# Two-layer graph attention: the first layer's value products split over two column tiles of 64 queries

## What is computed

```python
kc = k.reshape(B, H, Nc, CHUNK, Dh)          # B 8, H 4, Nc 8, CHUNK 256, Dh 64
vc = v.reshape(B, H, Nc, CHUNK, Dh)
scores = jnp.einsum('bhnd,bhjcd->bhnjc', q, kc) / sqrt(Dh)
scores = jnp.clip(scores, -10.0, 10.0)
scores = jnp.where(mask == 0, -10.0, scores)
attn = jax.nn.softmax(scores, axis=-1)
ctx = jnp.einsum('bhnjc,bhjcd->bhnd', attn, vc)
```

## Time and profile before

| what | value |
|---|---|
| runs of the kernel before | 4877.83 and 4884.79 us, median 4881.31 |
| profiled execution, first to last instruction (span) | 4877.6 us |
| TensorE busy, matmuls / weight loads | 4739.8 us (97%) / 4347.8 us (89%) |
| VectorE / ScalarE / GpSimd busy | 84% / 61% / 15% |
| granted TensorE clock, mean | 0.995 of 2.4 GHz |
| first layer | from the start to about 3390 us |
| second layer | the rest, about 1490 us |

### The profile page before, as it was taken

How to read it: one execution, slowest core, us unless ns; L and a number is a source line. 1 busy time by engine, 2 the same in 40 slices (tenths; PEclk the granted TensorE clock), 3 DMA queues, 4 the chain that set the end, 5 groups by cost and what they waited for, 6 DMA issues and landing times. The chain is left out here.

```text
span 4877.6 us, 136121 instructions
## 1 busy us (share of the span) xinstructions
PE 4739.8 (97%) x56349; PEld 4347.8 (89%) x56349; DVE 4078.2 (84%) x9728; ACT 2977.2 (61%) x3317; POOL 738.5 (15%) x613
## 2 busy tenths in 40 slices
PE   7999999999999999999999999997899999999999
PEld 5998899898899988989888998996899999999998
DVE  5888788787788877878877887787899999999999
ACT  5444444444444444444444444443899999999998
POOL 3121121111121211211211211011000110100100
PEclk9999999999999999999999999999999999999999
DMA  5100100001010001000001000010321221221221
GB/s 113 53 18 18 31 27 19 23 18 27 19 31 18 18 23 27 27 15 27 20 17 32 27 18 18 21 36 22 105 79 31 76 79 31 76 79 31 76 66 38
DMA packets 173916, 186.82 MB, mean 38 GB/s; under 512 B 7520, under 2 KB 157408, under 8 KB 173152
## 3 DMA queue, kind: packets, MB, share of 16 engines
q1 hardware_dynamic: 166192, 159.49, 11.9%
q0 software_dynamic: 7088, 18.36, 1.6%
HBM read 110.43 MB, written 38.03 MB: 30 GB/s over the span
## 5 line engine op out<-in xcount | busy, mean ns | idle before, releaser
L785 ACT ACTIVATE slot<-slot,shift 128x1024 f32<-128x1024 f32 x1024 | 1113.5, 1088 | 1568.7 <-PE slot L638 1568.7
L648 PEld LDWEIGHTS outs<-v_s,probs 128*128 128x128 f32 x16384 | 1974.5, 192 | 106.3 <-issue 29.7
L648 PE MATMUL outs<-v_s,probs 128*128 128x128 f32 x16384 | 1988.3, 275 | 0.0
L921 DVE SCALAR_TENSOR_TENSOR probs<-slot,bound 128x1024 f32<-128x1024 f32 x1024 | 1250.3, 1223 | 368.9 <-ACT slot L785 365.3
L1555 ACT ACTIVATE u<-s_all,d_sign 128x1024 bf16<-128x1024 f32 x1024 | 1117.1, 1138 | 56.9 <-PE sums L1456 39.5
L637 PE MATMUL slot<-q_hl,k_hl 128*128 128x512 f32 x2048 | 895.2, 437 | 18.5 <-DVE probs L921 9.9
L638 PE MATMUL slot<-q_hl,k_hl 128*128 128x512 f32 x2048 | 802.7, 392 | 0.0
L941 DVE SCALAR_TENSOR_TENSOR ctx_sum<-outs,inv,ctx_sum 128x64 f32<-128x64 f32 x3584 | 770.0, 278 | 31.7
L1452 PE MATMUL sums<-x_mixed,u 128*128 128x130 f16 x8192 | 785.5, 219 | 3.7 <-issue 3.5
L1456 PE MATMUL sums<-x_mixed,mask 128*128 128x65 f16 x8192 | 759.4, 193 | 5.5 <-issue 5.5
L1687 DVE TENSOR_TENSOR u<-u,mask 128x1024 f16<-128x1024 bf16 x1024 | 694.3, 689 | 76.6 <-ACT u L1555 67.6
(11 more groups left out here) (156 smaller groups left out, 3678.5 us busy)
## 6 DMA issues: line engine op xcount, KB each, us to landing
q_hl<-q_hl SPq DMA_DIRECT2D x128, 256.0 KB, 3.7
s_all<-s_turned SPq DMA_DIRECT2D x64, 512.0 KB, 5.7
x_q_s<-in_x SPq DMA_DIRECT2D x32, 512.0 KB, 4.6
x<-y SPq DMA_DIRECT2D x32, 512.0 KB, 3.2
t_o_s<-x SPq DMA_DIRECT2D x16, 1024.0 KB, 5.5
out<-t_o_s SPq DMA_DIRECT2D x16, 1024.0 KB, 6.9
x_q_s<-x SPq DMA_DIRECT2D x28, 512.0 KB, 5.8
probs<-in_adj POOLq DMA_DIRECT2D x12, 512.0 KB, 8.4
```

The source lines that it names most:

```text
L648: end = nc.tensor.matmul(outs[i % OUTS][:, q, :], probs[:, i % PROBS, r, q * P:(q + 1) * P], v_s[:, c * JC + r, h * E1:h * E1 + P], start= ...
L785: nc.scalar.activation(slot[:, :, :], slot[:, :, :], ACT.Exp, bias=shift[:, 0:1], scale=SCALE).then_inc(act_done, 1)
L921: nc.vector.scalar_tensor_tensor(probs[:, i % PROBS, :, :], spot(kind, "step", s, i)[:, :, :], P_LOW, bound[:, (i // H) % 2, :, :], ALU.ma ...
```

## The change

Each of the 8 products of `values` becomes two. The stationary operand is now 64 of the 128 queries, and the result goes to partitions 0 to 63 of `outs` for the first half and 64 to 127 for the second, which are two column tiles of TensorE's array. Each of the two streams the same 128 columns of `v_s`, as the one did before (`V_COLS` = `P` = 128). What is computed, where it lands and all waits and signals stay as they were; the signal is still on the last matmul of the step. The number of matmuls of `values` doubles, in the order tile, half of the chunk, half of the queries.

```diff
+V_COLS = P
...
-        v_w = H * E1 + P - E1
+        v_w = H * E1 + V_COLS - E1
...
                     for q in range(IT):
                         for r in range(JC):
-                            end = nc.tensor.matmul(outs[i % OUTS][:, q, :], probs[:, i % PROBS, r, q * P:(q + 1) * P],
-                                                   v_s[:, c * JC + r, h * E1:h * E1 + P],
-                                                   start=(r == 0), stop=(r == JC - 1))
+                            for g in range(2):
+                                rows_of = slice(g * D, (g + 1) * D)
+                                end = nc.tensor.matmul(outs[i % OUTS][rows_of, q, 0:V_COLS],
+                                                       probs[:, i % PROBS, r, q * P + g * D:q * P + (g + 1) * D],
+                                                       v_s[:, c * JC + r, h * E1:h * E1 + V_COLS],
+                                                       start=(r == 0), stop=(r == JC - 1))
                     end.then_inc(probs_used, 1)
```

## The result

The changed kernel takes 5186.51 us (runs of 5185.37 and 5187.66), the kernel before 4881.31: a ratio of 1.0622, 95% interval 1.0602 to 1.0642. That is slower by 305 us. The profiled execution is the one of 5185.37 us; its span is 5183.5.

What follows compares the result with a forecast made beforehand. The prediction took TensorE's matmul stream in the first layer as the bound. 4881 + 68 (an extra slot per step) + 336 (array emptying at grouping changes) = 5285 us, +8.3%; range 4830 to 5830.

Steps and rivals of the forecast that it cites:

- TensorE bounds the first layer, the load sets the pass: First layer: TensorE's stream sets the time; loading 128 fp32 weights decides each value pass, 0.1117 us, by 3 ns over streaming.
- The halves' streams overlap: Value products: both array halves work side by side, so 32 passes need the time of 16 slots of 0.109 us.
- rival C: Value passes: the two halves don't overlap at all, +1.70 us per step, 6623 us; chance 0.12.
- 17 slots per step: Value block: in-order starts and no overlap on one half add a slot; +0.066 us per step, +68 us.
- Loads, at nothing: Value weight loads: 64-column loads hide behind another stream; bounds 0 and 0.15 us per step, taken as 0.
- Rival B: Value loads wait for the matmul before them: +0.90 us per step, 5803 us without emptying; chance 0.11.
- Regrouping, 0.328 us per step: Between scores and values: the array empties at two grouping changes per step, 0.162 + 0.166 us, +336 us in all.
- Rival A, no emptying: Between scores and values: grouping travels with each instruction, costing no drain; 4949 us, or 4837 without a lost slot; chance 0.34.
- The range of the likeliest case: Whole kernel, halves side by side with emptying, chance 0.40: 5090 to 5454 us.
- half of the tails missing: Grouping changes between scores and values: the assumption given for the 5090 us lower end, only part of the emptying paid.

Runs made afterwards that it cites:

- the pairs: Scores of two steps issued, then values of two steps, on the kernel before with nothing split: 4927.73 us, ratio 1.0092.

## Why the prediction was right, and where it was not

The forecast was 5285 us (+8.3%) with a range of 4830 to 5830; measured were 5187 (+6.2%). The sign and the range held, the mechanism (two halves side by side, paid for with two changes of grouping per step) held, and the forecast was 98 us too high. That it came this near is in part luck: inside the largest term two errors cancel.

- *TensorE bounds the first layer, the load sets the pass.* Right: 65 columns in place of 128 change nothing while the load is whole (+0.2%).
- *The halves' streams overlap* (against rival C). Right: 32 passes in 16 slots, and 0.109 us per slot in the run with the block twice.
- *17 slots per step.* Wrong, and this is the failed step: "Matmuls start in order here" does not hold between the halves. The block has 16 slots, as the timeline shows. The term was +0.066 us per step; measured, it is 16 x (0.109 - 0.1117) = -0.04, or -0.048 with the 0.1087 us used in the expectations. The difference, 0.11 us x 1024 = some 115 us, is the whole error and a little more.
- *Loads, at nothing.* Right: pairs start 0.109 us apart, as if no load were there, except for the 0.05 us of each block's first pair, and with 65 columns the interval falls to 0.058 us, which loads one behind the other would not allow (0.118 by the prediction's 59 ns each). Rival B, loads waiting for the matmul before them in program order, is out.
- *Regrouping, 0.328 us per step.* The size came out well, 0.346, which is 354 us in place of 336. The makeup was off. I had priced the whole time until the last results land (0.162 us from scores to values, 0.166 back, beyond the usual next start) and let the load stand ready. The rows show a shorter emptying, 0.09 us in either direction (0.32 - 0.23 and 0.20 - 0.11), and a load that is not ready: it starts only afterwards, 0.05 us for 64 columns and 0.1 for 128. Two errors of opposite sign, and the near hit of the term is luck.
- *Rival A, no emptying*, on which I had put 0.34, rested on L719, a 64-column operand right behind whole value passes without a gap. The profile after shows what that row is:

```profile
3686.97 0.11 PEld L723 LDWEIGHTS slot<-ident,sd 128*64 128x64 f32 x1 [0.17 <-issue]
3686.97 0.30 PE L723 MATMUL slot<-ident,sd 128*64 128x128 f32 x1
```

The same transpose now follows split passes and has the gap of a change of grouping. So it runs on the whole array in spite of its 64 columns, and it was no evidence on tiles. I had named that doubt and should have weighed it more.
- *The range of the likeliest case.* Its lower end of 5090 does not follow from its own words: half of the tails missing gives 4949 + 168 = 5117. The result lies above both.

The drain that the Trainium skill names (TensorEngine Tiling (Array Packing), Key Properties) is what the runs show: 0.173 us for each change of the mode on average, with the load behind it, and nothing for a change of tile within it. The Trainium skill's figure for overlapping tiles holds in kind too (TensorE: Matmul & The Clock Gate, Part 3, starts some 4 ns apart): in the changed kernel two tiles run at once, with starts 6 or 7 ns apart. That page's statement there that matmuls are strictly first in, first out, without reordering, is not what the halves' order showed: with 16 passes for one half in a row, the second half began 6 ns after the first half's 13th pass, ahead of its last three.

The instruction queue grew from 7.52 MB to 9.60, 2.1 MB more, as worked out, with no effect to be seen.

## What to carry to other kernels

Column tiles pay in two ways, shorter weight loads side by side and streams side by side, and each change between tiled and whole use of the array cost the same here with one, two or four per step and whatever stood between: 0.17 us on average, some 0.15 into the tiles and 0.20 out of them. So count the changes before the products: here a split that leaves the stream at full length gains 3 ns per slot and loses two changes per step, while the same split with the streams cut to what is read gains 8%. And find out first whether load or stream sets the pass, since cutting the one that does not is worth nothing by itself. Then look at what the shorter stage meets: with 65 columns the other engines' waits and the clock took back 100 of the expected 490 us.

## What the runs showed that I had not expected

- Passes for the two halves are taken out of order within a short look-ahead: the order half by half within a tile costs 51 us, with 16 passes of one half in a row 1382 us.
- The loads of the two halves overlap as well: 32 passes of 65 columns start within 0.92 us, 0.06 us per pair, where a load of 64 fp32 weights takes an estimated 0.055.
- Splitting one tile of four is slower (5226 us) than splitting all (5187).
- With 65 columns the granted clock falls: 0.991 to 0.994 on the whole array, 0.990 to 0.993 on the tiles and 0.982 or 0.983 there in pairs, against 0.994 or 0.995 in the kernel before. On the whole array that is what the profiled run lost.
- Left open: how the 100 us that 65 columns on tiles fell short divide among VectorE, the copy of the queries and the clock, and the part of the 46 us of the pairs that does not lie at the strips' starts.
